# Excess tiles one loop group earlier, finer waits before the first expert product, the last tile's product in two halves, five warm-up products

## The reference, cut to what matters

```python
q, k, v = split(einsum('btc,oc->bto', x, w_attn)); q, k = rope(q), rope(k)       # 32 heads of 16
attn = softmax(where(causal, q k^T / sqrt(16), -inf))                            # 1024 x 1024 for each head
y = attn v + gating * softmax(q ak^T / sqrt(512)) av                             # 10 adapter keys
x = layernorm(x + y w_proj^T)
base = x base_w^T + base_b
probs = softmax(x router_w^T); topw, topi = top_k(probs, 2); combine = scattered topw / sum(topw)
delta = einsum('bse,bsr,eor->bso', combine, x A^T, B)                            # (combine (x) hidden) @ B_T
out = layernorm(x + base + 0.5 * delta)
```

## Time and profile before

| | us |
|---|---|
| median of 3 runs (lowest, highest) | 813.16 (812.86, 813.42) |
| profiled execution | 813.01 |
| its span | 811.2 |
| PE busy in the span | 793.2 |
| DVE busy in the span | 689.6 |
| ACT busy | 439.2 |
| POOL busy | 303.8 |
| granted TensorE clock, mean | 0.999 |

### The profile page before, as it was taken

The page is one execution under the profiler, slowest core; times in us unless marked ns, Lnnn a source line. Parts: engine busy times, 40 slices in busy tenths (PEclk is TensorE's granted clock), DMA queues, the critical chain, the costliest instruction groups (busy, mean ns, idle before and its releaser), DMA issues.

```text
span 811.2 us, 15794 instructions
## 1 busy us (share of the span) xinstructions
PE 793.2 (98%) x5262; PEld 533.1 (66%) x5262; DVE 689.6 (85%) x2100; ACT 439.2 (54%) x843; POOL 303.8 (37%) x387
## 2 busy tenths in 40 slices
PE   9999999999999999999999999999999999999996
PEld 6788876876545555454555555555458888888885
DVE  4874767678899999999999999999688888888877
ACT  5333322323479988888998888998851111111110
POOL 0213121222223452535436454555442734435321
PEclk9999999999999999999999999999999999999999
DMA  8316183364613444343354445351421101011111
GB/s 292 113 42 200 38 238 100 98 189 107 158 44 68 106 99 93 79 103 89 81 122 107 85 101 114 79 122 43 125 77 47 53 26 52 26 52 42 37 40 39
DMA packets 44097, 75.51 MB, mean 93 GB/s; under 512 B 13372, under 2 KB 14844, under 8 KB 44028
## 3 DMA queue, kind: packets, MB, share of 16 engines
q1 hardware_dynamic: 44028, 74.64, 35.4%
HBM read 48.30 MB, written 21.23 MB: 86 GB/s over the span
## 4 chain that ended last, share of the span: by engine, by line
PE 80%; DVE 8%; ACT 5%; issue 2%; DMA 1%; SPq 1%; POOL 0%; DVEq 0%
PE bank L1854 16%; PE bank L1738 11%; PE bank L1723 11%; PE bank L550 11%; PE bank L552 10%; PE bank L551 10%; ACT pt L1109 4%; PE bank L1667 2%; PE bank L2001 2%; PE bank L1733 1%; PE bank L1683 1%; PE bank L1749 1%; DVE b_low L1369 1%; PE bank L1734 1%; DMA ks<-k_parts 1%
## 5 line engine op out<-in xcount | busy, mean ns | idle before, releaser
L1109 ACT ACTIVATE pt<-bank 128x512 f32<-128x512 f32 x576 | 305.1, 621 | 52.8 <-PE bank L1723 49.9
L1249 DVE CUSTOM_DVE_ANT_0 bank<-bank,cmask 128x256 f32<-128x256 f32 (+3 forms) x456 | 202.8, 491 | 22.0 <-PE bank L1738 20.5
L1723 PE MATMUL bank<-qs,ks 50*128 50x512 f32 (+3 forms) x768 | 206.2, 377 | 1.1
L1738 PE MATMUL bank<-ks,qs 48*128 48x512 f32 (+3 forms) x712 | 190.0, 391 | 2.2 <-DMA ks<-k_parts 1.2
L1738 PEld LDWEIGHTS bank<-ks,qs 48*128 48x128 f32 x712 | 101.0, 185 | 90.7 <-DVE mx L1252 28.1
L1854 PE MATMUL bank<-pt,vb 128*32 128x512 f32 (+3 forms) x1536 | 157.0, 496 | 0.2 <-ACT pt L1109 0.2
L876 POOL TENSOR_SCALAR_AFFINE_SELECT pt<-pt 128x512 f32<-128x512 f32 (+1 forms) x160 | 85.3, 553 | 157.8 <-ACT pt L1109 157.8
L1723 PEld LDWEIGHTS bank<-qs,ks 50*128 50x128 f32 x768 | 114.9, 185 | 36.4 <-ACT pt L1109 25.0
L1252 DVE TENSOR_REDUCE mx<-bank 128x1 f32<-128x512 f32 x200 | 130.6, 679 | 1.4 <-PE bank L1738 1.1
L795 POOL TENSOR_TENSOR part<-rope,part 128x1024 fp32r<-128x1024 f32 x16 | 38.2, 2389 | 164.1 <-ACT part L967 164.1
L921 POOL TENSOR_TENSOR g<-comb,hr 128x1024 f32<-128x1024 f32 x16 | 30.5, 1906 | 110.5 <-DVE comb L1490 105.0
(11 more groups left out here) (194 smaller groups left out, 1535.2 us busy)
## 6 DMA issues: line engine op xcount, KB each, us to landing
qs<-q_parts SPq DMA_DIRECT2D x34, 256.0 KB, 3.9
ks<-k_parts SPq DMA_DIRECT2D x34, 256.0 KB, 4.4
q_parts<-part SPq DMA_DIRECT2D x32, 256.0 KB, 3.5
k_parts<-part SPq DMA_DIRECT2D x32, 256.0 KB, 3.5
qs<-q_parts SPq DMA_DIRECT2D x34, 128.0 KB, 5.0
ks<-k_parts SPq DMA_DIRECT2D x34, 128.0 KB, 3.3
yv<-yts SPq DMA_DIRECT2D x128, 32.0 KB, 2.3
rspread<-dens SPq DMA_DIRECT2D x64, 64.0 KB, 2.3
```

The lines of the kernel that those rows point to most:

```text
L1109: act.activation(pt[k % PT_BUFS][:, h], score_out(g, c), ACT.Exp, scale=float(HD) ** -0.5).then_inc(S("exp_done"), 1)
L1249: last = ve.tensor_tensor_reduce(blk, blk, cmask[:, BANK - nk * P:], 1.0, NEG, ALU.add, ALU.max, mx[m][:, 0, h, qt:qt + 1])
L1723: last = pe.matmul(score_out(g, c)[:, col:col + n_], ks[slot_of(g)][r0:r0 + KX, h // 2, kb * P:(kb + 1) * P], qs[slot_of(g)][r0:r0 + KX, h ...
L1738: last = pe.matmul(out[:, col:col + nk * P], qs[slot][r0:r0 + KR, pr, qt * P:(qt + 1) * P], ks[slot][r0:r0 + KR, pr, k0 * P:(k0 + nk) * P] ...
```

## The change

**Excess from group 0.** EXCESS_FROM becomes 1, so loop group 0, which makes the maxima for group 1, also uses excess tiles. POOL makes `nq` for it ahead of the loop, behind the 10th value copy of the head stage's last tile. In group 0 four tiles (numbers 8, 13, 22 and 29) get a second product by nq, ACT gets four copies, POOL four masks, and DVE four joined reads (tiles 12, 17, 32 and 35) in place of eight reads. The chunk at which the copy stands is worked out for each group (`excess_chunk`), since group 0 places its slots otherwise. SLOT_CLEARED loses its entry 1, one small memset of DVE.

**Waits by piece.** `delta(0)` waited for all 12 split weight pieces ahead of its first product. Now it waits for 8, and ahead of each of its last four steps for one more.

**The last tile.** `last_delta` computes tile 15's delta in two halves of 256 columns, each in a PSUM buffer of its own, 48 products in place of 24. DVE adds and measures each half by itself (`add_last_half`), and the aggregation takes both halves. On DVE `add_base(15)` now stands behind `lo_g(15)`.

**Warm-up.** WARM_UP becomes 5.

```diff
-EXCESS_FROM = 2
+EXCESS_FROM = 1
-SLOT_CLEARED = [0, 1]
+SLOT_CLEARED = [0]
-WARM_UP = 6
+WARM_UP = 5
+def slots_at(g):
+    return FIRST if g else [first_slots(c) for c in range(SCORE_BANKS)] + [SLOTS]
+def excess_chunk(g, slot):
+    return EXCESS_LAG + max(c for c in range(SCORE_BANKS) if slots_at(g)[c] <= slot)
...
             def negate_q(g):
                 gp.wait_ge(S(f"qk{(g + 1) % 3}"), 16 * LOADS * ((g + 1) // 3 + 1))
-                gp.wait_ge(S("excess_copied"), excess_before(g))
-                gp.wait_ge(S("diag_masked"), len(MASKED) * (g - 1) + sum(last_chunk(i) <= NEGATE_AT for i in MASKED))
+                if g > 0:
+                    gp.wait_ge(S("excess_copied"), excess_before(g))
+                    gp.wait_ge(S("diag_masked"), len(MASKED) * (g - 1) + sum(last_chunk(i) <= NEGATE_AT for i in MASKED))
...
+            gp.wait_ge(S("value_full"), NV * (TILES - 1) + 10)
+            negate_q(0)
             for g in range(G):
                 gp_group(g)
...
                     for i, slot in enumerate(slots_with(excess, g)):
-                        if EXCESS_CHUNK[slot] == c:
+                        if excess_chunk(g, slot) == c:
                             copy_excess(g, i)
...
+            def add_last_half(n):
+                t, m = NTC - 1, (NTC - 1) % 2
+                cols = slice(n * C // 2, (n + 1) * C // 2)
+                ve.wait_ge(S("ff_full"), t + 1 + n)
+                ve.wait_ge(S("x1_biased"), t + 1)
+                ve.tensor_tensor(xb[m][:, cols], xb[m][:, cols], last_out(n), ALU.add).then_inc(S("ff_summed"), 1)
+                ve.wait_ge(S("ff_summed"), t + 1 + n)
+                ve.bn_stats((sm[:, 16:22], sm[:, 22:28])[n], xb[m][:, cols]).then_inc(S("out_measured"), 1)
...
-                ve.wait_ge(S("out_measured"), t + 1)
-                ve.bn_aggr(sm[:, 30:32], sm[:, 22:28]).then_inc(S("out_aggregated"), 1)
+                ve.wait_ge(S("out_measured"), t + 2)
+                ve.bn_aggr(sm[:, 30:32], sm[:, 16:28]).then_inc(S("out_aggregated"), 1)
...
                 if not sure and j == NTC + 1:
                     lo_g(j - 2)
+                    add_base(j - 2, m)
...
-                if sure or 3 <= j <= NTC:
+                if sure or 3 <= j < NTC:
                     add_base(j - 1, 1 - m)
             drive_tiles(ve, ve_c)
-            add_ff(NTC - 1, (NTC - 1) % 2)
-            measure_out(NTC - 1, (NTC - 1) % 2)
+            for n in range(2):
+                add_last_half(n)
...
+            def last_delta():
+                t, m = NTC - 1, (NTC - 1) % 2
+                pe.wait_ge(S("ff_summed"), t - 1)
+                high, low = expanded(t)
+                for n in range(2):
+                    cols = slice(n * C // 2, (n + 1) * C // 2)
+                    for c_ in range(8):
+                        if n == 0 and c_ % CC == 0:
+                            pe.wait_ge(S("g_low"), t + 1 + c_ // CC)
+                        wbh, wbl = ((wbh0, wbl0), (wbh1, wbl1))[c_ // CC]
+                        last = three(pe, last_out(n), high[:, c_], low[:, c_], wbh[:, c_ % CC, cols], wbl[:, c_ % CC, cols],
+                                     c_ == 0, c_ == 7)
+                    last.then_inc(S("ff_full"), 1)
             def delta(t, m):
...
-                pe.wait_ge(S("cweight_low"), 3 * CC)
+                if isinstance(t, int) and t == 0:
+                    pe.wait_ge(S("cweight_low"), 2 * CC)
...
-                    if isinstance(t, int) and t == NTC - 1 and c_ == CC:
-                        pe.wait_ge(S("g_low"), t + 2)
+                    if isinstance(t, int) and t == 0 and c_ >= CC:
+                        pe.wait_ge(S("cweight_low"), 2 * CC + c_ - CC + 1)
...
-                if sure or j >= 3:
+                if sure or 3 <= j <= NTC:
                     delta(j - 2, m)
+                if not sure and j == NTC + 1:
+                    last_delta()
```

More of the change, by code:

```diff
@@ L249 @@
 EXCESS_USES = [use_of(_g, n) for _g in range(G) for n in slots_with(excess, _g)]
-EXCESS_CHUNK = {n: EXCESS_LAG + max(c for c in range(SCORE_BANKS) if FIRST[c] <= n) for n in slots_with(excess, EXCESS_FROM)}
-assert len(EXCESS_CHUNK) == HG and all(max_tile(n)[0] == 1 for n in EXCESS_CHUNK)
+assert len(slots_with(excess, EXCESS_FROM)) == HG and all(max_tile(n)[0] == 1 for n in slots_with(excess, EXCESS_FROM))
 def reads_before(use):
@@ L476, in x_bank, with last_out @@
             return half(FF_BANK[1] if isinstance(t, int) and t == 0 else X_BANK)
+        def last_out(n):
+            return half((FF_BANK[(NTC - 1) % 2], X_BANK)[n])[:, 0:C // 2]
         def router_of(t):
@@ L1859, in pe_group @@
             def pe_group(g):
-                slots = FIRST if g else [first_slots(c) for c in range(SCORE_BANKS)] + [SLOTS]
+                slots = slots_at(g)
                 for c in range(SCORE_BANKS):
```

## The result

The changed kernel takes 815.15 us in the median of 20 runs, the kernel before 812.86 in the median of 20. The ratio is 1.0036, 95% interval 1.0021 to 1.0051. It is slower: the whole interval lies above the 0.2% that a measurement can tell from no change. I had said 812.4 and no change, with a range up to 813.7.

The account below looks back on a forecast made before the run. PE was taken to bound the kernel, group 0 included. From the profiled 813.01 us, +0.68 (excess), -0.55 (waits), -0.80 (last tile) and 0 (warm-up) gave 812.34, stated as 812.4 us; range 810.9 to 813.7.

Parts of the forecast that it names:

- Excess on PE: Loop group 0: three of four added nq products lengthen PE's stretch, the fourth costs nothing; +0.68 us.
- DVE beside PE: Loop group 0: joined reads save DVE some 2.5 us, which counts for nothing while PE leads; bound -0.4.
- Rival (1): DVE leads group 0, so saved reads shorten it: 809.9 us, or 811 in part; chance 0.17 in full or part.
- Rival (3): Group 0: mode switches rule and the excess products hide entirely; 811.7 us, chance 0.12.
- Waits by piece: First expanded product: PE starts earlier, but most of the stall returns as a wait for x1; -0.55 us.
- rival (4): The -0.55 at delta(0) is lost in a later DVE wait, group 0 pays in full; 813.2 us, chance 0.22.
- Last tile: Kernel's end: earlier PE start, and only the second half's addition and statistics stand behind the products; -0.80 us.
- rival (2): Last tile: weight loads lead the halved products, 9.1 us in place of 5.6; total 815.5 us, chance 0.04.
- Warm-up: Kernel's start: one product less is taken up by PE's longer wait for DVE at 30.93; 0, +-0.1 us.
- The memset: Small DVE memset dropped with the excess edit: it lies beside PE, so no cost or gain was counted.
- The last step of the sum: From 812.34 to the forecast 812.4, as the profiled run lies 0.15 us under the median of 813.16.

Follow-up runs that it names:

- e8: The kernel before with the excess edit alone and one empty instruction more at the start of DVE's list: 813.16 us, ratio 1.0004.
- e5: The changed kernel with one empty instruction more at the start of DVE's list: 811.66 us, ratio 0.9986 to the kernel before.
- e4: The kernel before with the piecewise waits and the last tile's halves, without the excess edit, six warm-up products: 811.58 us, ratio 0.9985.
- e10: The kernel before with the piecewise waits at the first expanded product alone: 812.02 us, ratio 0.9991.
- e1: The kernel before with five warm-up products in place of six, nothing else: 812.84 us, ratio 1.0001.
- e6: The kernel before with one empty instruction moved from the start of DVE's list to SP's: 815.61 us, ratio 1.0053.
- e12: The kernel before with POOL's last mask of each group held until mneg is written and group 7's joining of maxima repeated six times: 815.06 us, ratio 1.0036.
- e2: The changed kernel with six warm-up products again: 815.08 us, ratio 1.0042 to the kernel before.
- e7: The changed kernel with POOL's last mask of each group held until mneg is written: 812.01 us, ratio 0.9990 to the kernel before.

## Why the prediction was wrong

**Excess on PE: right in the trace.** +0.67 for +0.68, as three of the four nq products lengthened their stretch; the 0.1 lost in group 1 was in no term. Over whole runs it may be less: +0.28 by e8, and e5 is only 0.08 above e4, which has no excess edit.

**DVE beside PE: right.** 2.6 us less work, nothing gained from it. Rival (1), that DVE leads group 0, fell: e8 is not faster, and PE's window is full. Rival (3), that the excess products hide entirely, fell with the +0.67.

**Waits by piece: right.** -0.53 in the trace, and the new wait of 1.11 us at the forecast place; -0.86 in the medians of e10. The shift was not lost again, as rival (4) had it: the stage still had it at the tail (1.74 late in place of 2.33).

**Last tile: right, a little small.** -0.91 for -0.80. The products of 256 columns are 0.12 apart, so rival (2), weight loads in the lead, fell. PE started at once behind tile 14's last product, 0.23 later, where I had left 0.24. DVE's halves cost 0.45 as interpolated. Together the two terms were -1.35 in the sum and -1.31 in e4.

**Warm-up: right as far as can be told.** e1 is at the kernel before's time. PE's wait at 30.93 is 0.89 us in e1, in place of 0.49; in both traces the clock comes up at 7.48. The wait of the changed kernel is no proof, since with six products it was between 0.40 and 1.11 in other traces:

```profile
31.60 0.47 PE L1635 MATMUL bank<-ident,pat 80*128 80x80 f32 x4 [1.05 <-DVE pat L1190]
```

**The memset: wrong.** "The memset that goes lies beside PE" was the step that failed, a term put at nothing because of where its work lies in time. As work it is worth nothing, as I said. As an entry of DVE's list it moved everything behind it by one place, and the joining for group 7, a spot where DVE has no reserve, came 0.36 us late and ran into POOL. PE stood still for 1.64 us, which cost the loop 1.5 in the profiled execution, and with the low clock behind it in some executions the median came to 3.5 us above that of the same kernel with an empty instruction put back (e5). I priced what instructions do and not where they stand. None of the rivals had it, nor the bounds, and the range was cut to the sum of terms in the stages that the edits touch; the loss lies 140 us behind the last touched group of the loop and 230 us ahead of the next edit.

**The last step of the sum.** 812.34 and the 0.15 between the profiled run and the median make 812.5, not 812.4; it changes nothing. Without the loss the number would have been off the other way: e5, at 811.66, lies below the 811.9 from which I counted the forecast.

**A margin was not looked at.** In the kernel before, mneg ends 0.02 to 0.14 us into POOL's mask at every joining from group 1 on, in most by 0.07 to 0.09, and at six of these fifteen a multiplication or addition of 1.28 us follows within 0.12 us. Rows of the timeline at any joining show it. At such an edge 0.36 us of delay on DVE cost 1.5 us (the changed kernel and e6), and a term for it would have widened the range upwards.

What stays open: why the same standstill is followed by a low clock in some executions and not in others, why the one at 613.5 us is followed by none, and how long the low clock then lasts. The traces at hand show 0 us (the changed kernel, e6, e12) and 3.41 us (e2), and the mean clocks of other runs point to longer ones; no trace of a run of over 815.2 us was kept, so that the low clock stands behind the standstill in those runs too is argued from e5, e7 and e12. That the place in the list decides was shown by moving it (e5, e6). That it is the border of a block is argued from the transfers, which move with it: the delayed instruction starts ahead of the transfer, so no row shows what DVE waited for, and that other borders are hidden was not tested.

## What to carry to other kernels

Before an edit is priced at nothing, look for the place in each period of the loop where two engines come within some tenths of a us of a collision, since the edit may cost what that place costs; here a wait on POOL that cost nothing took the risk away. Where a tuned kernel gets slower, or spreads, far from every edit, add or take one empty instruction on the engine that is late there before looking for a mechanism in the edit. A standstill of PE of 1.3 to 1.6 us had its price twice at one place of the loop, by its length and, in some executions, by a half clock behind it, and one of 1.67 us in the last stage had not; so a single profile can miss most of it: read the clocks of all runs.

## What the runs showed of the hardware

- One instruction more or less on DVE, with no work in it, moved the median by 3.5 us (815.15 to 811.66) and by 2.7 (812.88 to 815.61).
- DVE took 0.45 to 0.46 us in place of 0.10 between its last read of maxima and the joining that waits for it, in the five kernels whose traces have 959 instructions of DVE ahead of that joining, and 0.10 in the eight with 960 whose joining was left as it was.
- A TENSOR_SCALAR of 32 columns on DVE with one input took 0.64 us behind POOL's mask of 0.64, a SCALAR_TENSOR_TENSOR 1.21 behind POOL's multiplication of 1.26: until the other engine was done, in place of 0.18 and 0.19.
- Behind a standstill of PE of 1.64 us in the loop, 1.43 us of full work came at clock 1.00, and then 3.41 us at 0.50 (e2). In the changed kernel's trace 8.75 us behind the same standstill were at 1.00, and in the kernel before 9.84 us behind one of 1.67 us in the last stage.
- With no collision and no gap, a standstill of PE of 1.34 us at the same place in the loop left five of eleven runs at a mean clock of 0.998 or 0.999 and brought six down to between 0.996 and 0.991 (e12).
- Products of 256 columns with a weight load each follow at 0.120 us, those of 512 at 0.23.
